# Five held value units go back into the loop of the third cross attention, and both dense expert layers get three weight buffers, the first with stationary weights

## The reference, cut to what matters

```
# L0 cross attention: only the mean of the context rows is used
x += [x_norm, mean(ctx)] @ W + b
# L0 ffn, 8 experts, F = 704, every token through every expert
scores = xt @ Wg.T ; the best 2 of 8 keep their score as weight w, the others get 0
gate = silu(xt @ W1[e].T) ; up = xt @ W2[e].T ; y_e = (gate * up) @ W3[e].T
x += sum_e w[:, e] * y_e
# L2 cross attention, 16 heads of 16
q = x_norm Wq + bq ; k = ctx Wk + bk ; v = ctx Wv + bv
x += softmax(q k^T / 4, masked) v Wo + bo
# L2 ffn, 8 experts, F = 1024, every token through every expert
y_e = gelu(xt @ w_up[e].T) @ w_down[e].T ; out = sum_e w[:, e] * y_e ; x += norm(out) + xt
```

## Time and profile before

| | |
|---|---|
| median of three runs | 1585.85 us |
| the profiled execution's own time | 1592.37 us |
| its span | 1590.6 us |
| TensorE (PE) busy | 1505.8 us, 95% |
| VectorE (DVE) busy | 961.3 us, 60% |
| ScalarE (ACT) busy | 945.2 us, 59% |
| mean granted TensorE clock | 0.986 |
| DMA | 273.46 MB, mean 172 GB/s |

### The profile page before, as it was taken

The page is one execution under the profiler, slowest core; times in us unless marked ns, Lnnn a source line. Parts: engine busy times, 40 slices in busy tenths (PEclk is TensorE's granted clock), DMA queues, the critical chain, the costliest instruction groups (busy, mean ns, idle before and its releaser), DMA issues.

```text
span 1590.6 us, 34028 instructions
## 1 busy us (share of the span) xinstructions
PE 1505.8 (95%) x13910; PEld 1116.0 (70%) x13910; DVE 961.3 (60%) x1836; ACT 945.2 (59%) x1442; POOL 9.6 (1%) x22
## 2 busy tenths in 40 slices
PE   6989999899999999999998989999999999998899
PEld 5756578666777767776766876777777777776664
DVE  5512322647767778778875215776767676767631
ACT  3212032228888788888883105887777777778711
POOL 0000000000000000000000000000000000000000
PEclk9989999899999999999999999999999999999999
DMA  9476854355535254435312556443434333423336
GB/s 394 167 300 235 325 208 177 137 208 211 189 125 177 94 210 155 162 117 186 136 52 114 206 224 222 148 166 119 152 120 147 117 140 117 141 94 127 141 149 271
DMA packets 56455, 273.46 MB, mean 172 GB/s; under 512 B 6640, under 2 KB 6896, under 8 KB 49392
## 3 DMA queue, kind: packets, MB, share of 16 engines
q1 hardware_dynamic: 56304, 271.32, 46.3%
HBM read 162.64 MB, written 5.90 MB: 106 GB/s over the span
## 4 chain that ended last, share of the span: by engine, by line
PE 78%; DVE 7%; DMA 5%; ACT 5%; issue 5%; SPq 0%; POOL 0%; DVEq 0%; ACTq 0%
PE T L880 14%; PE O L903 9%; PE S L866 8%; PE O L880 7%; PE T L838 6%; PE T L851 5%; PE S L701 4%; PE O L838 3%; PE S L1222 3%; PE O L1251 3%; PE T L696 2%; ACT sc L1337 2%; PE O L701 2%; DVE sc L1792 2%; PE S L975 2%
## 5 line engine op out<-in xcount | busy, mean ns | idle before, releaser
L1792 DVE CUSTOM_DVE_ANT_0 sc<-S,mask_bias,small 128x896 f32<-128x896 f32 x336 | 377.5, 1148 | 45.9 <-PE S L866 45.9
L1337 ACT ACTIVATE sc<-sc,small 128x1792 f32<-128x1792 f32 x168 | 300.1, 1787 | 2.5 <-DVE small L1792 1.0
L1323 ACT ACTIVATE pT<-T 128x512 f32<-128x512 f32 x365 | 212.1, 598 | 87.4 <-PE T L880 87.4
L880 PE MATMUL T<-consts,sc 128*128 128x128 f32 x1558 | 235.1, 281 | 4.7 <-ACT sc L1337 3.1
L903 PEld LDWEIGHTS O<-pT,arena 128*32 128x32 f32 x6272 | 164.8, 110 | 74.8 <-issue 72.3
L880 PEld LDWEIGHTS T<-consts,sc 128*128 128x128 f32 x1558 | 169.9, 141 | 62.3 <-issue 40.0
L903 PE MATMUL O<-pT,arena 128*32 128x128 f32 x6272 | 194.4, 274 | 9.0 <-ACT pT L1323 9.0
L866 PE MATMUL S<-keys,q 64*128 64x512 f32 (+1 forms) x896 | 151.1, 414 | 10.1 <-DVE small L1792 9.9
L1758 DVE COPY pT<-T 128x512 f32<-128x512 f32 x152 | 104.8, 690 | 75.4 <-PE T L880 74.4
L1323 ACT ACTIVATE pT<-O 128x512 f32<-128x512 f32 x195 | 116.6, 598 | 50.5 <-PE O L880 50.5
L838 PE MATMUL T<-ctx_in,packs 128*128 128x448 f32 x316 | 133.4, 547 | 1.1 <-issue 1.1
(11 more groups left out here) (384 smaller groups left out, 1835.2 us busy)
## 6 DMA issues: line engine op xcount, KB each, us to landing
keys<-keys_hl SPq DMA_DIRECT2D x224, 448.0 KB, 4.4
ctx_in<-in_ctx_cols SPq DMA_DIRECT2D x46, 896.0 KB, 5.4
wide<-in_ctx_rows SPq DMA_DIRECT2D x14, 896.0 KB, 4.6
wide<-in_up_L0f SPq DMA_DIRECT2D x8, 1408.0 KB, 8.1
sc<-in_ctx_cols SPq DMA_DIRECT2D x10, 896.0 KB, 5.6
wide<-in_up_L2f SPq DMA_DIRECT2D x8, 1024.0 KB, 6.6
wide<-in_down_L2f SPq DMA_DIRECT2D x8, 1024.0 KB, 5.5
wide<-in_up_L3f SPq DMA_DIRECT2D x4, 2048.0 KB, 8.1
```

Of the source, the lines that this page charges most:

```text
L880: last = nc.tensor.transpose(ring(plan, u)[:, t * P:(t + 1) * P], weights_of(2 * m + i)[:, b * P:(b + 1) * P], ident)
L1323: nc.scalar.activation(pT2[:, g * BANK:(g + 1) * BANK], ring(plan, u), ACT.Copy).then_inc(s["t_act"], 1)
L1337: nc.scalar.activation(weights_of(n), weights_of(n), ACT.Exp, bias=n_best[c % 2][:, h:h + 1], scale=-1.0, accum_out=l_new[c % 2][:, h:h + ...
L1792: V.tensor_tensor_reduce(weights_of(n)[:, i * HC:(i + 1) * HC], S4f[:, n % 2 * 2 * BANK:n % 2 * 2 * BANK + HC], mask_bias[:, i * HC:(i + 1 ...
```

## The change

It does four things. (1) `WHOLE` is chunk 4 alone: units 2 to 6 of chunk 6 are no longer made in L0a and L0f's norm, but in the loop of L2x over chunk 5. Where they stood, `warm` stands, and some waits go. (2) The write of the held units, now 17 in two transfers, is issued by SP right after L0a's pack, when the fifth `AFTER` unit is taken; on SP it stands ahead of L0f's pack and first expert loads. (3) L0f gets `gated_dense`: stationary weights, output turned, no transposes. The 704 gate and 704 up columns are laid out as 11 tiles of 128 (tile 5 holds the last 64 of both). (4) L0f and L2f keep three experts' weights (`expert_cols`), and their loops on SP are written out.

```
-WHOLE = (4, 6)
+WHOLE = 4
+HELD_BUFFERS = {"L0f": 3, "L2f": 3}
+        def expert_cols(layer, e, part):
+            n = HELD_BUFFERS[layer]
+            m = KD * (2 if layer in GATED else 1) * FF[layer]
+            size = m + len(tiles(layer)) * D
+            at = e % n * (size if n == 3 else 3 * KD * 1024)
+            return wide[:, at:at + m] if part == 0 else wide[:, at + m:at + size]
 # SyncE
             def load_first(layer):
-                for e in range(2):
+                for e in range(HELD_BUFFERS[layer]):
                     ...
                     load_pack(layers[1])                      # in L0x
+                    sp.wait_ge(s["held_taken"], len(PASSING))
+                    sp.wait_ge(s["after_taken"], len(AFTER))
+                    sp.dma_start(held_out[:, 0:IN_ARENA], held_a).then_inc(s["held_out"], 16)
+                    sp.dma_start(held_out[:, IN_ARENA:len(HELD)], held_b).then_inc(s["held_out"], 16)
-                    if layer == "L0f":
-                        dump_held()
-                    with sp.Fori(1, E // 2) as n:
                     ...
+                    for e in range(n, E):
+                        sp.wait_ge(s["g_ready"], per * (e - n + 1))
+                        load_up(layer, e)
+                        sp.wait_ge(s["y_ready"], e - n + 1)
+                        load_down(layer, e)
 # TensorE
-                elif layer == "L0f":                          # norm: now warm(T2[:, 0], 11)
-                    after(9, S4[:, 2])
-                    warm(T2[:, 0], 4)
-                    after(2, S4[:, 1])                        # norm2
+                    warm(T2[:, 1], 5)
-                elif layer == "L0a":                          # tail: now warm(S4[:, 0], 5)
-                    after(8, S4[:, 1])
-                    pe.wait_ge(L["L0x"]["after_taken"], 3)    # qkv
-                    after(3, T2[:, 1]); after(4, O2[:, 1]); after(5, S4[:, 3], 2)
+                    after(2, T2[:, 1]); after(3, O2[:, 1]); after(4, S4[:, 3], 2)
-                        after(6, T2[:, 1], 4)                 # before qblk
-                        after(7, O2[:, 1], 5)
-                        pe.wait_ge(L["L0x"]["after_taken"], 6)
+                        pe.wait_ge(L["L0x"]["after_taken"], len(AFTER))
+                        warm(O2[:, 1], 11)
+            def gated_dense(layer):
+                def up(e):
+                    w = expert_cols(layer, e, 0).rearrange("p (k n) -> p k n", k=KD)
+                    pe.wait_ge(s[f"up_in{e % 3}"], 16 * (e // 3 + 1))
+                    if e: pe.wait_ge(s["act_done"], e)
+                    for t in range(6):
+                        last = product(S4f[:, t * P:(t + 1) * P], w[:, :, t * P:(t + 1) * P], xT)
+                    last.then_inc(s["g_ready"], 1)
+                    if e: pe.wait_ge(s["h_ready"], e)
+                    for t in range(5):
+                        last = product(S4f[:, 1024 + t * P:1024 + (t + 1) * P], w[:, :, (6 + t) * P:(7 + t) * P], xT)
+                    last.then_inc(s["g_ready"], 1)
+                def down(e):
+                    pe.wait_ge(s[f"down_in{e % 3}"], 16 * (e // 3 + 1))
+                    pe.wait_ge(s["h_ready"], e + 1)
+                    if e >= 2: pe.wait_ge(s["y_taken"], e - 1)
+                    for t, rows in tiles(layer):
+                        last = mm(O2[:, b, 0:D], hidden(b)[0:rows, t, :], w[0:rows, t, :], ...)
+                up(0)
+                for e in range(1, E):
+                    up(e); down(e - 1)
+                down(E - 1)
 # ScalarE, per expert: silu of 640 columns, silu of 64 rows x 128, copy of 64 rows x 128 -> act_done
 # VectorE, per expert: 64 rows x 128 product, 128 x 640 product -> h_ready, then
+                    V.scalar_tensor_tensor(yacc, O2[:, e % 2, 0:D], wts[:, e:e + 1], yacc, ALU.mult, ALU.add)
```

More of the change, by code:

```diff
@@ L46 @@
 GATED = ("L0f", "L3f")
+UP_TILES = 11
+HELD_BUFFERS = {"L0f": 3, "L2f": 3}
 def tiles(layer):
@@ L138 @@
 EARLY = 1
-WHOLE = (4, 6)
-KEPT = {"L2x": [0 if c == 1 else 7 if c in WHOLE else 2 for c in range(7)], "L3x": [0] * 7}
+WHOLE = 4
+KEPT = {"L2x": [0 if c == 1 else 7 if c == WHOLE else 2 for c in range(7)], "L3x": [0] * 7}
 KEY_STEPS = [(hf, nb) for hf in range(KD) for nb in range(KEY_UNITS)]
@@ L1032, in down @@
                     for t, rows in tiles(layer):
-                        last = mm(O2[:, b, 0:D], hidT[0:rows, t, :], w[0:rows, t, :], start=(t == 0),
-                                  stop=(t == tiles(layer)[-1][0]))
+                        last = mm(O2[:, b, 0:D], hidden(b)[0:rows, t, :], w[0:rows, t, :], start=(t == 0), stop=(t == 5))
                     last.then_inc(s["y_ready"], 1)
[L1037 to L1053, removed]
@@ L1055, in experts @@
                 if layer == "L0f":
                     pe.wait_ge(L["L0x"]["after_taken"], len(AFTER))
[L1057 to L1062, removed]
+                up(0)
+                for e in range(1, E):
+                    up(e)
+                    down(e - 1)
+                down(E - 1)
@@ L1205, in _ @@
                     done("pe", product(O2[:, 0, 0:E], xT, pk(layer, "gate", KD)), f"{layer}.logit")
-                    (dispatched if layer == "L3f" else dense if layer == "L2f" else experts)(layer)
+                    (dispatched if layer == "L3f" else dense if layer == "L2f" else gated_dense)(layer)
                 elif layer == "L1x":
@@ L1403, in dispatched, with gated_dense @@
                         .then_inc(s["t_act"], 1)
-            def experts(layer):
+            def gated_dense(layer):
                 s = L[layer]
[L1407 to L1413, removed]
-                        .then_inc(s["act_done"], 1)
-                    act.wait_ge(s["t_ready"], 2 * e + 2)
-                    full = [t for t, rows in tiles(layer)[4:] if rows == P]
-                    last = nc.scalar.activation(hidT[:, 4:4 + len(full), :].rearrange("p t n -> p (t n)"),
-                                                T2[:, 1, 0:len(full) * P], ACT.Copy)
-                    for t, rows in tiles(layer)[4 + len(full):]:
-                        last = nc.scalar.activation(hidT[0:rows, t, :], T2[0:rows, 1, t % 4 * P:(t % 4 + 1) * P],
-                                                    ACT.Copy)
-                    last.then_inc(s["t_act"], 1)
-                with act.Fori(0, E // 2) as n:
-                    for b in range(2):
-                        expert(2 * n + b)
+                for e in range(E):
+                    act.wait_ge(s["g_ready"], 2 * e + 1)
+                    if e:
+                        act.wait_ge(s["h_ready"], e)
+                    nc.scalar.activation(gated[:, 0:5 * P], S4f[:, 0:5 * P], ACT.Silu)
+                    nc.scalar.activation(gated[0:HR, 5 * P:6 * P], S4f[0:HR, 5 * P:6 * P], ACT.Silu)
+                    nc.scalar.activation(gated[0:HR, 6 * P:7 * P], S4f[HR:P, 5 * P:6 * P], ACT.Copy) \
+                        .then_inc(s["act_done"], 1)
             def dense(layer):
@@ L1686, in dispatched, with gated_dense, add_up @@
                 dve.wait_ge(s["y_ready"], E // 2 + 1)
[L1688 removed]
+            def gated_dense(layer):
                 s = L[layer]
[L1690 to L1693 removed]
+                def add_up(e):
                     dve.wait_ge(s["y_ready"], e + 1)
[L1696 removed]
+                    V.scalar_tensor_tensor(yacc, O2[:, e % 2, 0:D], wts[:, e:e + 1], yacc, ALU.mult, ALU.add) \
+                        .then_inc(s["y_taken"], 1)
@@ L1717, in experts @@
-                expert(0, 0, True)
-                expert(1, 1)
-                with dve.Fori(1, E // 2) as n:
-                    for b in range(2):
-                        expert(2 * n + b, b)
-                add_up(E - 1, 1)
+                    if e >= 2:
+                        dve.wait_ge(s["y_ready"], e - 1)
+                    V.tensor_tensor(h[0:HR, 5 * P:6 * P], gated[0:HR, 5 * P:6 * P], gated[0:HR, 6 * P:7 * P], ALU.mult)
+                    dve.wait_ge(s["g_ready"], 2 * e + 2)
@@ L2091, in _ @@
                     need(dve, "dve", f"{layer}.weights")
-                    (dense if layer == "L2f" else experts)(layer)
+                    (dense if layer == "L2f" else gated_dense)(layer)
                     if layer == "L2f":
```

148 lines of the change are left out of this document (54 added, 94 removed).

## The result

Seven runs of the changed kernel on the chip: 1577.12 us median (1574.25 to 1581.37), against 1586.58 (1582.47 to 1587.38) for seven of the kernel before. The ratio (time over that of the kernel before, measured beside it) is 0.9945 with a 95% interval of 0.9933 to 0.9958, so 6.7 to 10.6 us less. Forecast was a time 14.6 us under that of before, 1571.2: the range (1565 to 1580) holds the time, but a third of the gain is missing. The profiled execution took 1574.64 us, span 1573.0.

The account below looks back on a forecast made before the run. TensorE was taken as the bound, with 78% of the chain of waits. Terms 8.3 (L2x), -1.5 (L0a), -16.1 (L0f) and -5.3 (L2f) sum to -14.6 us, from the median 1585.85 to 1571.2; range 1565 to 1580.

Parts of the forecast that it names:

- L2x, +8.3: In L2x's loop over chunk 5, five added units cost 1.66 us each with nothing hiding them: +8.3 us.
- L0f on TensorE, -17.1: In L0f, stationary weights without transposes take 7.81 us per expert, eight experts 62.5 us against 79.6: -17.1 us.
- L0f's weights, +1.0: In L0f, with the write ahead of the first expert loads, TensorE waits for weights by narrow margins: +1.0 us.
- queue rival: In L0f, the write ahead of first loads costs 7.5 us instead of 1.0, total 1577.8 us; chance 0.15.
- L2f, -5.3: In L2f, a third buffer removes waits for up weights and a slow up, 56.3 against 61.7 us: -5.3 us.
- buffer rival: L2f's waits come from DMA rate, not lead, so it gains about 1 us: 1575.5 us; chance 0.08.
- L0a, -1.5: In L0a, removed units let the tail's turning start earlier, 1.9 us gained, 0.4 given back to low clock: -1.5 us.
- The sum against the median: Whole kernel: the profiled execution's -14.6 us was subtracted from the runs' median, 1585.85, giving 1571.2 us.
- weight-load rival: In L0f's up, 352 weight loads don't hide, 201 ns a matmul instead of 112: 1602.5 us; chance 0.03.
- free-units one: In L2x, the units cost nothing because something else bounds the pair: 1562.9 us; chance 0.03.

Follow-up runs that it names:

- write_late: Changed kernel with the held units' write back at its old place on SP, behind the first experts' weights and L1x's pack; three buffers kept: ratio 0.9955.
- l2f_two: Changed kernel with two weight buffers in L2f instead of three: 1580.01 us, ratio 0.9958.
- before_rep: The kernel before, unedited, run and profiled once more: median 1586.04 us, ratio 1.0.
- units_only: Kernel before with only chunk 6's five units moved into L2x's loop, 17 units held and written at the old place: 1593.22 us, ratio 1.0052.
- stream_three: Changed kernel with L0f's products as before (weights stream, transposes), keeping three buffers, early write and written-out loops: ratio 0.9994.
- l0f_two: Changed kernel with two weight buffers in L0f instead of three, the write still early: ratio 0.9955.
- two_late: Changed kernel with two weight buffers in L0f and the held units' write at its old place: ratio 0.9994.
- hold22: Changed kernel with all 22 units held again, five in other free memory, written in two further transfers after the fourth expert's weights: 1569.17 us, ratio 0.9884.
- hold22b: Kernel with all 22 units held and three buffers, the unit of L0a's tail moved to L0f's norm: 1570.17 us, ratio 0.9892.

## Why the prediction was right, and 5 us off

**L2x, +8.3: right.** Measured +8.1, and the five pairs to a hundredth (47.90 for 47.89). Two stretches that differ in one thing gave the price better than any duration could.

**L0f on TensorE, -17.1: right within 1 us.** 7.89 us per expert for 7.81 (an up takes 5.01, 114 ns a matmul, for 112), and from first up to last down 63.3 us for 62.5. ScalarE's and VectorE's work on an expert lay beneath TensorE's, as foreseen. In all L0f gave 16.2 us in the first pair of profiles and 15.1 by the means, forecast 16.1. By the table above the gain has two parts: 5.7 us come from the form of the products, and the other 9.4 mostly from the one long wait (5.4 to 6.9 us) and the slow up behind it (1.9 to 3.0 us over its 4.9).

**L0f's weights, +1.0: right, by a narrow margin.** No wait at all. The sum at 0.406 MB per us held: up(0) was put at 75.5, up(1) at 81.0, up(2) at 86.5 and up(3) at 96.7; they landed at 75.44, 80.70, 86.16 and 95.15. TensorE began on up(0) at 75.79 and on up(1) at about 80.8, so the first two had tenths of a us to spare, as the forecast said. The early write turns out to be worth 1 us or less beside the third buffer (write_late), no more than the low clock in that profile. The queue rival did not come. Its total, 1577.8, lies nearer to the measured 1577.12 than the forecast does, but that is chance: no row of L0f waits for weights. The figure of the Trainium skill (about 358 GB/s, "DMA: Bandwidth & Descriptors", section "Where 436 GB/s comes from") would have foretold a wait. This trace disagrees: it shows 434 GB/s from 75 to 81 us, when only loads were left.

**L2f, -5.3: the term that was most mis-sized.** I took the one execution's 61.7 us as the cost of two buffers. 3.0 us of it are (l2f_two), 3.6 by the means of three; the rest was a stretch of low clock behind the longest wait in that execution alone. The mechanism was right, the size was that of one draw. The buffer rival is out: the waits are gone.

**L0a, -1.5: right by the means (-1.9), but for another reason.** The stage varies by 3.7 us between executions of one kernel, 27.22 to 30.90, with the low clock in it or not. The executions in which it had none are before_rep with 27.22 and two of the changed kernel with 26.70: what the removed units give at full clock is 0.5 us. The 1.9 us that the forecast read from the tail were mostly the low clock's: at full clock the turning begins 0.2 us behind VectorE with the after unit in place. So the stretch of low clock, priced there at 0.4, was nearly the whole term.

**The sum against the median: the step that I did not see.** The forecast said that the profiled execution lay 6.5 us over the median and used its differences all the same. What made it slow was partly in the touched stages, so the sum counted it as gain. By the means of three profiles the four touched stages give -12.5 for the forecast -14.6: 1.7 of the missing 5 us are L2f's and 1.0 are L0f's, and L0a and L2x give 0.6 back. Two stages with no edit in them nearly cancel: L3a's -1.0, and L2a's +1.1, which is low clock. That stretch in L2a stands in all three profiles of the changed kernel, in units_only, stream_three and l0f_two, and not in write_late, two_late, l2f_two, hold22 and hold22b (23.94 each). Whether the change makes it more frequent stays open.

The other 3 us lie between profiles and runs: the means of three profiles say -12.2 where the runs say -9 (6.7 to 10.6). The changed kernel's three profiled executions are among the quick ones of its spread: 1574.64, 1576.86 and 1574.80 us at mean clocks of 0.992, 0.991 and 0.992, against a mean of 1577.33 us at 0.990 for its seven runs, 1.9 us more. Of the kernel before, the first profiled execution is at the slow end. So the rest is again which executions were profiled.

Two sums of the prediction are off by 0.1 to 0.2 and change nothing: half of 3.45 times five is 8.6 and not 8.7, and 8 x 7.03 is 56.2, which leaves 5.5 for L2f and not 5.3.

**The weight-load rival** is out at 114 ns a matmul, and so is the free-units one.

## What to carry to other kernels

Before a stage's cost in one profile is taken as what an edit can save, split it into waits, work at full clock and work at low clock, and only trust the last part if a second execution shows it. Compare a stage between kernels by executions that had the same clock in it. When an edit needs memory and pays for it with work, look for other memory first: the whole price here, 8 us, was for 10 KB per partition that lay free elsewhere. A third buffer and an earlier place on the queue can cure the same wait; price each without the other before adding them.

## What the runs showed of the hardware

The spread of the changed kernel's runs is that of the granted clock. By its seven runs: mean clock 0.992 at 1574.25, 1574.64 and 1574.80 us, 0.991 at 1577.12, 0.989 at 1579.21 and 1579.90, 0.988 at 1581.37. Four thousandths of 1577 us are 6.3 us, and the times differ by 7.1. The stretches fall on a few places or miss them: L3a, which no edit touches, takes 11.84 to 11.85 us at full clock and 14.78 or 14.79 when it has 6.8 us of low clock. These are the windows of L3a in before_rep and in write_late, the granted clock is the third number from the end:

```profile
1505.50:1517.30 11.80, 11.16 (x92) 10.45 (x91) 4.63 (x13) 0.00 (x0) 1.09 (x2) 1.00 0.86 365
```

```profile
1499.10:1513.80 14.70, 14.16 (x92) 13.63 (x91) 4.61 (x13) 0.00 (x0) 1.10 (x2) 0.77 0.69 291
```

A write of 4.46 MB from SBUF to DRAM and the loads behind it on one queue moved at similar rates: 390 GB/s from 60 to 70 us, nearly all write, and 407 and 434 GB/s in the two windows after it. The loads did not overtake the write: it landed at 70.44 and 71.99, up(0) at 75.44.
